# A third weight matrix that gets a sum of squares and a scale of its own, inside the odd step, in a fused attention and experts kernel

## The reference

```python
x = x + jnp.tanh(g_xattn[0]) * _L0_xattn_ref(ctx_1024, _layernorm(x, axis=-1), L0_xattn_wq, L0_xattn_wk, L0_xattn_wv)
x = x + jnp.tanh(g_ffn[0]) * _L0_ffn_ref(_layernorm(x, axis=-1), L0_ffn_Wg, L0_ffn_W1, L0_ffn_W2, L0_ffn_W3)
# _L0_xattn_ref: softmax attention of a sequence's rows to the rows of its context
# _L0_ffn_ref: for the two experts with the highest scores of a row, summed with the scores as weights
gate = jax.nn.silu(jnp.einsum('td,ehd->teh', xt, W1))
up = jnp.einsum('td,ehd->teh', xt, W2)
y = jnp.einsum('teh,edh->ted', gate * up, W3)
```

## Time and profile before

| | us |
|---|---|
| median of 3 runs | 594.71 |
| profiled execution, its own time | 598.21 |
| its span in the trace | 596.50 |
| PE busy | 561.9 (94%) |
| DVE busy | 319.4 (54%) |
| ACT busy | 322.4 (54%) |
| POOL busy | 255.7 (43%) |
| start of the last step (15) in the trace | 164 |

### The profile page before, as it was taken

One profiled execution on the slowest core, in us unless ns is written; L12 is line 12 of the kernel. 1 busy time (PEld: TensorE's weight loads), 2 busy tenths in 40 slices (PEclk: granted clock), 3 DMA queues, 4 the chain that ended last, 5 costly groups with the idle time before them and its releaser, 6 DMA issues.

```text
span 596.5 us, 14490 instructions
## 1 busy us (share of the span) xinstructions
PE 561.9 (94%) x4625; PEld 490.0 (82%) x4625; DVE 319.4 (54%) x902; ACT 322.4 (54%) x458; POOL 255.7 (43%) x242
## 2 busy tenths in 40 slices
PE   7898989888888999989999999999999999999995
PEld 6687778777777899878998898898898998898783
DVE  3388799878978776842343334334334334333332
ACT  3678888888874554444353443444444435434441
POOL 4028647655555676643324323333233332432323
PEclk9898999999989999999999999999999999999999
DMA  7545877668522434542232332232332332222322
GB/s 253 184 127 179 282 232 253 206 229 257 158 93 102 104 95 93 148 97 43 50 57 38 47 65 38 46 66 37 46 62 42 49 50 53 42 40 43 49 40 27
DMA packets 52371, 61.49 MB, mean 103 GB/s; under 512 B 7632, under 2 KB 46160, under 8 KB 52304
## 3 DMA queue, kind: packets, MB, share of 16 engines
q1 hardware_dynamic: 34096, 38.14, 21.1%
q0 software_dynamic: 13296, 18.23, 17.8%
q10 hardware_dynamic: 4912, 4.20, 2.1%
HBM read 36.90 MB, written 23.66 MB: 102 GB/s over the span
## 4 chain that ended last, share of the span: by engine, by line
PE 59%; DVE 12%; DMA 9%; issue 8%; POOL 6%; ACT 4%; SPq 3%; POOLq 0%; ACTq 0%; DVEq 0%
PE psum L921 29%; PE psum L953 18%; DMA w_in<-in_W3T 7%; PE psum L806 5%; PE psum L930 4%; POOL rows_by_expert L567 3%; POOL out L602 2%; DVE w_lo L1055 2%; PE psum L849 2%; DVE w_lo L1048 2%; DMA xa<-in_x 1%; DVE xa L1143 1%; SPq L433 1%; ACT w_hi L676 1%; PE psum L939 1%
## 5 line engine op out<-in xcount | busy, mean ns | idle before, releaser
L602 POOL DMA_INDIRECT out<-w_in,id_s x71 | 128.9, 1816 | 236.7 <-ACT w_in L752 115.6
L921 PE MATMUL psum<-arena,w_hi 128*128 128x256 f16 x1408 | 211.3, 273 | 1.9 <-issue 1.5
L921 PEld LDWEIGHTS psum<-arena,w_hi 128*128 x1408 | 137.4, 98 | 18.7 <-issue 2.5
L921 PE MATMUL psum<-arena,w_lo 128*128 128x256 f16 x704 | 134.4, 273 | 0.0
L683 ACT ACTIVATE arena<-psum 128x1024 f16<-128x1024 f16 (+1 forms) x39 | 36.9, 947 | 106.9 <-PE psum L849 106.9
L1358 DVE SCALAR_TENSOR_TENSOR arena<-psum,h_unit,arena 128x1280 f32<-128x1280 f32 x32 | 49.6, 1550 | 63.4 <-PE psum L921 63.3
L567 POOL DMA_INDIRECT rows_by_expert<-xn2r,slot_i x64 | 72.9, 1138 | 18.4 <-issue 17.5
L921 PEld LDWEIGHTS psum<-arena,w_lo 128*128 x704 | 68.9, 98 | 8.0
L806 PE MATMUL psum<-arena 128*128 128x264 f32 x256 | 68.3, 422 | 1.6 <-DVE place L1112 0.5
L806 PEld LDWEIGHTS psum<-arena 128*128 128x128 f32 x256 | 50.8, 205 | 12.4 <-ACT arena L691 1.9
L728 ACT ACTIVATE arena<-psum,w_unscale 64x256 f32<-64x256 f32 x32 | 15.0, 467 | 85.0 <-PE psum L921 85.0
(11 more groups left out here) (192 smaller groups left out, 824.6 us busy)
## 6 DMA issues: line engine op xcount, KB each, us to landing
xa<-rows_by_expert SPq DMA_DIRECT2D x71, 136.0 KB, 2.2
w_in<-in_W1T SPq DMA_DIRECT2D x8, 704.0 KB, 4.7
w_in<-in_W2T SPq DMA_DIRECT2D x8, 640.0 KB, 4.8
w_in<-in_W3T SPq DMA_DIRECT2D x8, 640.0 KB, 5.6
arena<-in_ctxT SPq DMA_DIRECT2D x16, 256.0 KB, 6.1
xa<-in_x SPq DMA_DIRECT2D x16, 256.0 KB, 6.3
out<-xa ACTq DMA_DIRECT2D x16, 256.0 KB, 4.3
out<-w_in,id_s POOLq DMA_INDIRECT x71, 4.2
```

The costliest lines, as they stand in the source:

```text
L602: pool.indirect_dma_start(out=out[:, :], out_offset=bass.IndirectOffsetOnAxis(ap=id_s[:, t8:t8 + 1], axis=0), in_=y_s[:, t8 % 4, :], in_of ...
L921: ins = pe.matmul(flat_ps[:, j * N2:(j + 1) * N2], w12[w_part][:, c, bass.ds(e * (2 * H) + j * P, P)], xg_t[:, k, x_part, c, :], start=(q ...
```

## The change

Four edits are made.

1. W3's squares no longer stand behind W2's ahead of the odd step. They are a piece of their own (`squares3`) in the middle of the odd step, behind the normalized rows. Their sum over the partitions is a matmul of its own (`weight_sum3`) between the scores and the values, and goes to bank 3 of PSUM, where the product v stands too. Their scale is made by two small instructions of their own, behind the maxima of the scores. There are four new semaphores.
2. In slot 0 PE turns the last probabilities and does the fifth chunk of hidden features before it waits for step 14's output and makes the rank of sequence 9.
3. In slot 6 POOL issues the scatter of the last sequence ahead of the addition that stood before it.
4. ACT starts its three small loads (the router's weights and two gates) when wk has landed, and not at once.

```diff
@@ def rank_ps ... @@
-        ssq_ps = bank[7][:, 448:450]
+        ssq_ps = bank[7][:, 448:449]
+        ssq3_ps = bank[3][:, 448:449]
@@ gpsimd, slots @@
+                if i == len(AT_PAIR):
+                    scatter(B - 1)
                 if i >= 2 and pair(i - 2):
                     add_rows(i - 2, 1)
-                if i - 1 in AT_PAIR:
+                if i - 1 in AT_PAIR and i < len(AT_PAIR):
                     scatter(AT_PAIR[i - 1])
@@ scalar @@
+            act.wait_ge(s_wk, 16)
             act.dma_start(wg_s[:], WgT.rearrange("(c p) e -> p c e", p=P)).then_inc(s_wg_in, 16)
...
             def high3(e):
+                act.wait_ge(s_scale3, e + 1)
...
-                ins = act.activation(w12[0][:, :, u * H:(u + 1) * H].bitcast(BF16), w12_in[:, u % 2], ACT.Square,
-                                     accum_out=ssq[:, 0:1])
-                if u % 2 == 1:
-                    act.wait_ge(s_w3, 48 * e + 48)
-                    ins = act.activation(w3[0][:, :, e * D:(e + 1) * D].bitcast(BF16), w3_in[:], ACT.Square,
-                                         accum_out=ssq[:, 1:2])
-                ins.then_inc(s_sq, 1)
+                act.activation(w12[0][:, :, u * H:(u + 1) * H].bitcast(BF16), w12_in[:, u % 2], ACT.Square,
+                               accum_out=ssq[:, 0:1]).then_inc(s_sq, 1)
+            def squares3(e):
+                act.wait_ge(s_w3, 48 * e + 48)
+                at_least(act, s_ssq3, e)
+                act.activation(w3[0][:, :, e * D:(e + 1) * D].bitcast(BF16), w3_in[:], ACT.Square,
+                               accum_out=ssq[:, 1:2]).then_inc(s_sq3, 1)
@@ scalar, step n, behind norm_rows @@
+                if live(n) and k == 1:
+                    squares3(e)
@@ tensor @@
-                w = 1 + u % 2
-                pe.matmul(ssq_ps[:, 0:w], ones_f[:], ssq[:, 0:w], start=True, stop=True).then_inc(s_ssq, 1)
+                pe.matmul(ssq_ps, ones_f[:], ssq[:, 0:1], start=True, stop=True).then_inc(s_ssq, 1)
+            def weight_sum3(e):
+                pe.wait_ge(s_sq3, e + 1)
+                pe.wait_ge(s_v_copied, 2 * e + 2)
+                pe.matmul(ssq3_ps, ones_f[:], ssq[:, 1:2], start=True, stop=True).then_inc(s_ssq3, 1)
...
+                at_least(pe, s_half3, n // 2)
                 product(v_ps, ctx_s[:, k], wv_s).then_inc(s_v, 1)
...
                 product(sc_and_xw_ps, x_t, z_s).then_inc(s_sc, 1)
+                if k == 1:
+                    weight_sum3(n // 2)
@@ tensor, slot 0 @@
                             to_hidden(range(4), expert[u], k)
-                            pe.wait_ge(s_x2, B - 1)
-                            rank(IN_STEPS - 1)
                             turn_probs(B - 1)
                             pe.wait_ge(s_v_copied, B)
+                            pe.wait_ge(s_half3, E)
                             to_hidden(range(4, KF), expert[u], k)
+                            pe.wait_ge(s_x2, B - 1)
+                            rank(IN_STEPS - 1)
@@ vector @@
-                    half_exp = halves[:, k:1 + 2 * k, e]
-                    scales(half_exp, ssq_ps[:, 0:1 + k], w_scale[:, 0:1 + k], s_half, s_scale, n)
+                    scales(halves[:, k:k + 1, e], ssq_ps, w_scale[:, 0:1], s_half, s_scale, n)
@@ vector, behind maxima(n) @@
+                if live(n) and k == 1:
+                    dve.wait_ge(s_ssq3, e + 1)
+                    scales(halves[:, 2:3, e], ssq3_ps, w_scale[:, 1:2], s_half3, s_scale3, e)
```

More of the change, by code:

```diff
@@ L247, in gated_cross_attention_and_experts @@
         s_sq = sem("s_sq")
+        s_sq3 = sem("s_sq3")
+        s_ssq3 = sem("s_ssq3")
+        s_half3 = sem("s_half3")
+        s_scale3 = sem("s_scale3")
         s_ssq = sem("s_ssq")
@@ L980, in moe_step @@
                             to_hidden(range(4), expert[u], k)
+                            turn_probs(B - 1)
+                            pe.wait_ge(s_v_copied, B)
+                            pe.wait_ge(s_half3, E)
+                            to_hidden(range(4, KF), expert[u], k)
                             pe.wait_ge(s_x2, B - 1)
                             rank(IN_STEPS - 1)
-                            turn_probs(B - 1)
-                            pe.wait_ge(s_v_copied, B)
-                            to_hidden(range(4, KF), expert[u], k)
                             pe.wait_ge(s_lo12, 2 * E)
@@ L1191, in units @@
                 dve.wait_ge(s_half, B)
+                dve.wait_ge(s_half3, E)
                 dve.wait_ge(s_tanh, 1)
```

## The result

| | before | after |
|---|---|---|
| median, 20 runs each, us | 596.52 (592.69 to 599.91) | 592.83 (591.66 to 594.57) |
| ratio, 95% interval | | 0.9945 (0.9929 to 0.9961) |
| profiled execution, its own time | 598.21 | 591.74 |
| its span | 596.5 | 590.0 |

The change is 0.55% faster, 3.3 to 3.7 us. The forecast was 6.5 us and 588.2, its range ended at 592.5. The two *profiled* executions differ by just those 6.5. So there are two questions: did the steps come out as reckoned, and why do the medians differ by half as much.

The account below looks back on a forecast made before the run. Bound: a first-phase queue of waits around W3's squares, only DVE's stands counting as gain. Sum: 3.4 + 3.5 + 1.5 + 0.2 - 2.7 - 0.3 + 1.2 - 0.3 = 6.5 us off the median, 588.2; range 586.5 to 590.5, outer 585 to 592.5.

Parts of the forecast that it names:

- the new wait: DVE's second wait, for W3's sum ahead of the choice in choosing odd steps; choice 3.93 us behind DVE's first instruction, as before.
- step 1, without the start: First odd step: sum starts earlier, PE at full clock, DVE's residual 3.4 us earlier, 1.7 of it the clock.
- step 3 (0.94 - 1.35): DVE's stand of 0.94 us goes, but the clock falls behind W3's sum and the residual starts 1.35 later.
- steps 7 and 13: Odd steps with nothing normalized: DVE regains most of its stand for the values, 1.5 us less.
- step 9 (-1.35): DVE never stood here, so no gain; the clock falls behind W3's sum and costs 1.35 us.
- hand-overs: Between engines in the steps: 0.3 us taken off the gain for hand-overs laid without a gap.
- slots: Slot 6's last scatter starts some 4.9 us earlier, and the rows of slot 8 with it: 1.2 us gained, bounds 0 and 1.4.
- start: ACT's three small loads begin later, mostly hidden by DVE's stand for x: 0.3 us lost, bounds 0 and 1.5.
- The clock: PE waits at W3's sum and its clock falls in steps 3, 9 and 15: 2.7 us lost in 3 and 9.
- The squares were not the bound: Rival: DVE and ACT's ring is as long with the new wait; gain only 2.5 us, 592.2; chance 0.20.
- Rank 0: Slot 0: rank moved behind the turned probabilities; PE still waits 0.77 us for DVE's residual; gain 0, bounds 0 and 0.8.
- wrong if: Signs: steps 9 and 10 shrink by over a us, step 1 at half clock, or slots earlier by less than 3 us.

Follow-up runs that it names:

- scatter_alone: The kernel before with the edit of slot 6 alone (last scatter ahead of the addition), second kind of chip: 604.59 us, ratio 1.0051.
- before_again: The kernel before, unchanged, run and profiled a second time: 594.72 us.
- before_third: The kernel before, unchanged, run and profiled once more, on a chip of the second kind: 599.82 us.
- squares_early: The changed kernel with ACT's squares of W3 ahead of the normalized rows, not behind them: 585.69 us, ratio 0.9823.
- start_undone: The changed kernel with ACT's three small loads started at once, as before the change: 591.98 us, ratio 0.9916.
- rank_undone: The changed kernel with the rank of slot 0 where it stood before, on a chip of the second kind: 602.84 us, ratio 1.0039.

## Why the forecast was off, point by point

**The step that failed** is the last of the sum: "the same 6.5 off the median gives 588.2". The miss of 4.6 has two parts. The median of three runs, 594.71, was 1.8 below that of twenty. And the gain in medians is 3.7, not 6.5: the profiled execution of before was 1.7 over its median, that of after 1.1 under its own. By terms, the split gave 3.1 in a median where the sum had 5.6, and the three other edits 0.6 together where it had 0.9. Before's steps vary from one execution to the next (step 1 by 2.7, step 13 by 2.2), with the falls of the clock. Why the profiled execution was 1.7 over its median is not shown in full. It lost its clock in steps 1 and 3, as scatter_alone did (before_again in 3 and 13, before_third in 1, 3 and 13). Its step 15 was the longest of the four, 23.87 against 21.72 to 23.18, and its slots were 0.4 to 0.8 longer than in the three other profiles of the first kind with both slot edits left out.

**The mechanism that failed** is that of the new wait: "such a step is not shorter from there on, and gains only what DVE stood ahead of it". In step 3 that gave -0.4, and it measured -2.4. With the squares ahead of the normalized rows the same split is 7.1 faster.

**The terms, against the pair of profiles.** The sum of 6.5 was met, but by errors that cancel, which is luck:

| term | forecast | measured |
|---|---|---|
| step 1, without the start | 3.4 | 2.45 + 0.8 = 3.25 |
| step 3 (0.94 - 1.35) | -0.4 | -2.4 |
| step 5 | 1.06 | 1.03 |
| steps 7 and 13 | 1.5 | 1.0 |
| step 9 (-1.35) | -1.35 | 0.1 |
| step 11 | 1.48 | 1.67 |
| step 15 | 0.2 | 0.5 |
| hand-overs | -0.3 | in the steps |
| slots | 1.2 | 6.5 - 4.3 = 2.2 |
| start | -0.3 | -0.8 |

- Step 3. The way from DVE's first instruction to the choice was laid as 3.93 from the rows of step 11. In steps 5 and 9 it came to 3.71. In step 3 it was 44.30 to 50.04, 5.74, since the rows waited for POOL (1.3 beyond DVE's shift) and two of DVE's small instructions beside POOL took 0.56 and 1.16. The trace of before hid this: ACT had W3's squares to do in that time.
- The clock: forecast to fall in 3, 9 and 15, it fell in 3 and 15, and in 9, after the same 2.47, it fell in two of the seven profiles with that stand (1.7 us) and held in the pair's. That makes up for most of step 3. The reading under it, that the clock fell after 2.16 and not after 1.76, is no rule: it fell after 1.43 and 1.47 and held after 2.18 and 2.28 in other executions of the same program.
- "The squares were not the bound" had 0.20 and 592.2, the nearest number, by luck. It kept 1.7 of step 1, the part that is not the clock, and 1.2 of the scatter. In medians the split is 3.1, of which filling the stand alone, the clock, gives 2.6. The ring isn't as long as that either; squares_early takes 7.1 more out of it. The wait for the squares stayed, at another place.
- The slots: rows of slot 8 are started at 250.99 (259.76 before), POOL's last scatter at 242.00. The row of 1.18 in the earlier trace rows was 0.30 in before_again. The early scatter gave 1.2 and 1.7 between medians on the first kind, of which the profiles have 0.3 to 1.0 in the slots. On the second kind the sign turns, which no term or rival had.
- The start was mis-sized by 0.5: "DVE stands 4.74 for x" was no cover, since x itself landed 0.8 later. The Trainium skill (DMA: Bandwidth & Descriptors, Queues, rings and completion order) has each transfer engine go round its queues packet by packet, by which the loss would be nearer 1.5. start_undone bears out the direction, 0.85; no trace here shows the turns.
- Rank 0: not settled. Beside an early scatter it is 0 (rank_undone), beside a late one about 1 comes with it. The two new small instructions took 0.15 each in all eight odd steps, none 0.96, so the value taken was right. Four of the eight pairs ran beside an arithmetic instruction of POOL, as in step 5 (DVE, POOL):

```profile
70.68 0.15 DVE L1052 TENSOR_SCALAR w_scale<-halves 128x1 int32<-128x1 int32 x1
```

```profile
70.12 1.15 POOL L585 TENSOR_TENSOR xn2r<-arena,xn2r 128x512 f16<-128x512 f32 x1
```

As far as this form goes, the trace agrees with the Trainium skill (SBUF — State Buffer, Who interferes with whom), by which a DVE instruction with at most one SBUF input outside the two-port modes does not contend with GpSimd. The slow one of before had two elements a partition, so what made it slow stays open.
- Of the signs named ahead, all came but three: the clock behind W3's sum in step 9 held, PE's stand in steps 5 and 11 was 1.42, not 1.0, and DVE waited 0.45 there (1.0 forecast). "Over 2" in step 3 came as 4.08, where the sum had 2.3 to 2.5. None of the "wrong if" signs came, and the time was off all the same: they looked at the mechanism in one pair of traces, and the miss was in what a pair of traces stands for.

## What to carry to other kernels

Splitting a wait moves it to wherever the second half stands. Put the second half ahead of the next instruction on its engine that waits for others, not behind it: here that place was worth 7.1 us and the split itself 3.1. When several edits go in together, undo each alone and look at where the gain lies: that of slots 7 and 8 looked like the scatter's, and is there without it. And before a gain is laid off a median, see in a second profile of the kernel before which of its stands repeat; a stand whose clock falls in some executions only is worth the share of executions in which it does.

## What the runs showed of the hardware

- The same program on the same data keeps full clock in one execution and loses it in the next, and the length of PE's stand ahead does not order the two. In step 1 before, 1.85 held, 2.16 fell twice and 2.17 once; elsewhere 1.43 and 1.47 fell, 2.18 and 2.28 held; the 2.47 of step 9 held in the first profile of the changed kernel and fell in the second. Filling part of a stand of 2.16 made the median 2.6 faster and needed no other change.
- Chips differ in more than speed. On two of four, PE's instructions came with seven to nine gaps, most of 0.2 to 0.45, every 0.7 us over some 6 us of one slot, in all seven profiles with the early scatter, and not in the one profile without it. What these gaps are is open: the profile calls them "issue". They fall in a stretch where the transfer engines are busy for 0.77 of the time. The same edit was 1.7 us faster in one kernel on a chip of the first kind and 3.1 slower in another kernel on one of the second.
